# Softmax attention on one core: the scores of a head as two fp16 passes over projected queries and keys, in place of three passes over a folded product

## What is computed

```python
def _L1_attn_ref(hidden_states, w_q, w_k, w_v, w_o, rel_bias_table):   # 16 heads of 64
    q = shape(hidden_states @ w_q)
    k = shape(hidden_states @ w_k)
    v = shape(hidden_states @ w_v)
    scores = jnp.einsum('bhqd,bhkd->bhqk', q, k)
    scores = scores + position_bias
    attn = jax.nn.softmax(scores.astype(jnp.float32), axis=-1).astype(scores.dtype)
    ctx = jnp.einsum('bhqk,bhkd->bhqd', attn, v)
    return ctx.reshape(B, S, INNER) @ w_o
```

## Time and profile before

| quantity | value |
|---|---|
| median of three executions | 3229.51 us |
| the profiled execution, its own time | 3240.09 us |
| its span, first to last instruction | 3238.0 us |
| attention stage, about 1676 us to 3003 us of the span | 1327 us |
| busy in the span: TensorE, VectorE, ScalarE, GpSimd | 74%, 70%, 57%, 43% |
| mean granted TensorE clock | 0.903 |

### The profile page before, as it was taken

One profiled execution on the slowest core, in us unless ns is written; L12 is line 12 of the kernel. 1 busy time (PEld: TensorE's weight loads), 2 busy tenths in 40 slices (PEclk: granted clock), 3 DMA queues, 4 the chain that ended last, 5 costly groups with the idle time before them and its releaser, 6 DMA issues. The chain is left out here.

```text
span 3238.0 us, 66865 instructions
## 1 busy us (share of the span) xinstructions
PE 2386.1 (74%) x17707; PEld 1919.1 (59%) x17707; DVE 2265.8 (70%) x8247; ACT 1857.2 (57%) x4874; POOL 1401.3 (43%) x1366
## 2 busy tenths in 40 slices
PE   2217888384226787307868999999999999999587
PEld 2217676363225676305655877777777777778365
DVE  4325766685433666577977888888888888888697
ACT  2114444252213344235637988888888888889464
POOL 3553555302563555405532444444444444444365
PEclk9999999696558999758988999999999999999799
DMA  4133333312114333340000000000000000000000
GB/s 151 40 67 93 98 99 95 100 39 87 40 50 100 97 99 95 94 122 1 0 27 4 5 4 4 4 4 4 4 4 4 4 4 4 4 4 5 6 20 27
DMA packets 141736, 138.32 MB, mean 43 GB/s; under 512 B 17012, under 2 KB 127412, under 8 KB 140772
## 3 DMA queue, kind: packets, MB, share of 16 engines
q1 hardware_dynamic: 118932, 95.46, 9.8%
q0 software_dynamic: 17408, 35.82, 3.5%
q10 hardware_dynamic: 5200, 4.84, 0.5%
HBM read 59.31 MB, written 44.24 MB: 32 GB/s over the span
## 5 line engine op out<-in xcount | busy, mean ns | idle before, releaser
L2088 POOL TENSOR_TENSOR p_prob<-p_prob,p_inverse 128x512 f32<-128x512 f32 x512 | 533.3, 1042 | 797.0 <-DVE p_inverse L1912 797.0
L2005 ACT ACTIVATE p_prob<-p_neg,p_neg_max 128x256 f32<-128x256 f32 x1024 | 508.8, 503 | 40.2 <-DVE p_neg_max L1906 40.2
L1916 DVE SCALAR_TENSOR_TENSOR p_probT<-p_t_ps,p_probT 128x512 f16<-128x512 f32 x512 | 353.0, 689 | 195.1 <-ACT p_probT L2011 135.6
L883 ACT ACTIVATE p_e_hT<-p_e_h_ps,p_b 128x256 f32<-128x256 f32 x576 | 230.9, 474 | 352.9 <-PE p_e_h_ps L832 216.0
L997 POOL DMA_INDIRECT results_by_token<-p_e_result,p_e_slot x288 | 285.2, 990 | 309.6 <-DVE p_e_result L943 234.2
L706 POOL DMA_INDIRECT rows_by_expert<-p_r_z,p_r_target x256 | 249.4, 974 | 371.5 <-DVE p_r_z L561 258.2
L1906 DVE CUSTOM_DVE_ANT_0 p_neg<-p_s_ps,top_bias 128x256 f32<-128x256 f32 x1024 | 388.3, 416 | 0.8 <-ACT p_prob L2005 0.6
L2011 ACT ACTIVATE p_probT<-p_t_ps 128x512 f16<-128x512 f32 x512 | 304.9, 596 | 71.2 <-PE p_t_ps L2156 69.5
L841 PE MATMUL p_e_o_ps<-p_w,p_e_hT 128*128 x2304 | 308.2, 289 | 35.4 <-issue 22.7
L841 PEld LDWEIGHTS p_e_o_ps<-p_w,p_e_hT 128*128 128x128 f32 x2304 | 285.5, 201 | 55.9 <-issue 55.9
L2156 PE MATMUL p_t_ps<-top_ident,p_prob 128*128 128x128 f32 x2048 | 308.8, 273 | 7.0 <-POOL p_prob L2088 7.0
(11 more groups left out here) (266 smaller groups left out, 6157.3 us busy)
## 6 DMA issues: line engine op xcount, KB each, us to landing
p_e_affine<-p_affine SPq DMA_DIRECT2D x144, 192.0 KB
p_e_z<-rows_by_expert SPq DMA_DIRECT2D x144, 129.0 KB, 2.2
p_got<-results_by_token SPq DMA_DIRECT2D x64, 256.0 KB, 2.9
results_by_token<-p_e_result,p_e_slot POOLq DMA_INDIRECT x288
p_r_w<-in_w SPq DMA_DIRECT2D x2, 2048.0 KB, 7.6
p_w<-in_w SPq DMA_DIRECT2D x2, 2048.0 KB, 11.8
rows_by_expert<-p_r_z,p_r_target POOLq DMA_INDIRECT x256
p_reversed<-bias_by_distance ACTq DMA_DIRECT2D x2, 2048.0 KB, 17.1
```

What stands on the lines that cost most here:

```text
L1916: v.scalar_tensor_tensor(probT[k % 2][:, 1, :, :], t_ps[k % 2][:], PROB_SCALE, probT[k % 2][:, 0, :, :], ALU.mult, ALU.subtract).then_inc( ...
L2005: ins = act.activation(prob[k % PROBS][:, t, :], neg[k % 2][:, t, :], ACT.Exp, bias=neg_max[k % 2][:, t:t + 1], scale=-1.0, accum_out=tota ...
L2088: pool.tensor_tensor(prob[k % PROBS][:], prob[k % PROBS][:], inverse[k % PROBS][:].unsqueeze(2).to_broadcast([P, SEQ_TILES, SEQ]), ALU.mult)\
```

## The change

The folded matrix A and the operand gT are gone. Queries and keys are projected with the plain weights, two heads (a pair, 2 by 64 = 128 output rows) at a time: of a quad's eight projections, four are now Q and K of two pairs, four are the values as before. The banks and slots stay: `act_ps` takes Q0, Q1, V0, V2, `v_ps` takes K0, K1, V1, V3. The split into high and low parts and its two copies per projection stay too.

The scores of a head contract over 64 instead of 128. In `stacked` each head has its query high and low parts one above the other on 128 partitions, and its key high part twice. One pass of full height then gives high by high plus low by high; a second pass, of 64 rows, taken straight from `qkT`, adds high by low. The stacking is done by SyncE: four DMAs within SBUF (64 partitions by 512 fp16 columns, 64 KB) for Q and four for K of each pair, 16 a quad, 64 a group. SyncE waits for the copies out of PSUM before them, and TensorE waits at the first scores of each pair for `moved`, the semaphores of these DMAs. In the setup the 16 products for A and their copies are replaced by a split of the weights read from memory.

```diff
+FIRST_BANK = ((Q, 0), (Q, 1), (V, 0), (V, 2))
+SECOND_BANK = ((K, 0), (K, 1), (V, 1), (V, 3))
...
-        gT = [m.sb(f"gT{b}", [P, 2, QUAD, GN], F16) for b in range(2)]
+        qkT = [m.sb(f"qkT{b}", [P, 2, 2, QUAD_PAIRS, GN], F16) for b in range(2)]
+        stacked = [m.sb(f"stacked{b}", [P, 2, QUAD, GN], F16) for b in range(2)]
...
+            def move(of, pair, i, g):
+
+                here, there_ = qkT[g % 2], stacked[g % 2]
+                first, second = slice(0, D_HEAD), slice(D_HEAD, P)
+                for h, own in enumerate((first, second)):
+                    parts = (HIGH, LOW) if of == Q else (HIGH, HIGH)
+                    for part, to in zip(parts, (first, second) if h == 0 else (second, first)):
+                        sp.dma_start(there_[to, of, pair * 2 + h, :], here[own, part, of, pair, :]).then_inc(moved[of][pair], 16)
+
+            def stack_quad(i, g):
+
+                if not (first_group(i) and g < 2):
+                    sp.wait_ge(s_done, i * GROUP_UNITS + (g - 1) * UNITS)
+                    sp.sem_inc(carried, 1)
+                for pair in range(QUAD_PAIRS):
+                    sp.wait_ge(act_taken, g_ready(i, g, pair))
+                    sp.sem_inc(carried, 1)
+                    move(Q, pair, i, g)
+                    sp.wait_ge(v_taken, v_number(i, g, pair) + 1)
+                    sp.sem_inc(carried, 1)
+                    move(K, pair, i, g)
...
             for n in range(QUADS):
                 norms.raw(v, n * (TILES // QUADS), TILES // QUADS, x_res)
-                v.wait_ge(a_kept, 2 * n + 1)
-                v.scalar_tensor_tensor(a_low[:, a_heads(n), :], a_bank(n), A_SCALE, a_high[:, a_heads(n), :], ALU.mult, ALU.subtract).then_inc(a_kept, 1)
+            for of in (Q, K):
+                v.wait_ge(qk_split, 2 * of + 1)
+                v.scalar_tensor_tensor(wqk_low[:, of], wqk[:, of], A_SCALE, wqk_high[:, of], ALU.mult, ALU.subtract).then_inc(qk_split, 1)
...
+                pair = g * QUAD_PAIRS + n
+                return three_passes(out, (wqk_high[:, of, pair, :], wqk_low[:, of, pair, :]), (src[:, 0, :], src[:, 1, :]))
...
             def scores(i, k):
                 g, b, hd = quad_of(k), k % UNITS // QUAD, k % QUAD
-                if b == 0:
-                    pe.wait_ge(act_taken, g_ready(i, g, hd))
-                if k == UNITS:
-                    pe.wait_ge(key_ready, i * 16 + 16)
+                pair, half = hd // 2, slice(hd % 2 * D_HEAD, hd % 2 * D_HEAD + D_HEAD)
+                if b == 0 and hd % 2 == 0:
+                    for of in (Q, K):
+                        pe.wait_ge(moved[of][pair], (i * QUADS + (g + 1)) * 64)
                 if not early(i, k, 2):
                     pe.wait_ge(max_ready, i * GROUP_UNITS + (k - 1))
-                keys = zT if g == 0 else keyT
                 toks = slice(b * SEQ, (b + 1) * SEQ)
                 for t in range(SEQ_TILES):
                     rows = slice(b * SEQ + t * P, b * SEQ + (t + 1) * P)
-                    ins = three_passes(s_ps[k % 2][:, t, :], (gT[g % 2][:, 0, hd, rows], gT[g % 2][:, 1, hd, rows]),
-                                       (keys[:, 0, toks], keys[:, 1, toks]))
+                    pe.matmul(s_ps[k % 2][:, t, :], stacked[g % 2][:, Q, hd, rows], stacked[g % 2][:, K, hd, toks], start=True, stop=False)
+                    ins = pe.matmul(s_ps[k % 2][:, t, :], qkT[g % 2][half, HIGH, Q, pair, rows], qkT[g % 2][half, LOW, K, pair, toks],
+                                    start=False, stop=True)
                 ins.then_inc(s_done, 1)
```

More of the change, by code:

```diff
@@ L1639 @@
 A_SCALE = 2.0 ** 4
-G_SCALE = 2.0 ** 5
+QK_SCALE = 2.0 ** 5
 B_SCALE = 2.0 ** 4
@@ L1643 @@
 PROB_SCALE = 2.0 ** 15
-SCORE_SCALE = G_SCALE * Z_SCALE
+SCORE_SCALE = QK_SCALE * QK_SCALE
+QUAD_PAIRS = QUAD // 2
+Q, K, V = range(3)
+FIRST_BANK = ((Q, 0), (Q, 1), (V, 0), (V, 2))
+SECOND_BANK = ((K, 0), (K, 1), (V, 1), (V, 3))
 UNITS = GROUP_SEQS * QUAD
@@ L1789, in bias_attention @@
                                              for key in ("o_done", "o_kept", "o_turned", "o_added"))
-        a_done, a_kept, b_done, b_kept = m.sem("a_done"), m.sem("a_kept"), m.sem("b_done"), m.sem("b_kept")
+        qk_split, b_done, b_kept = m.sem("qk_split"), m.sem("b_done"), m.sem("b_kept")
+        moved = [[m.sem(f"{key}_moved{pair}") for pair in range(QUAD_PAIRS)] for key in ("q", "k")]
+        carried = m.sem("carried")
         high_ready, key_ready = m.sem("high_ready"), m.sem("key_ready")
@@ L1798, in bias_attention, with kept @@
         OUT_SCALE = 1.0 / (PROB_SCALE * VALUE_SCALE)
+        HIGH, LOW = range(2)
+        def kept(g, part, use):
+            of, n = use
+            return (val[g % 2][:, part, n, :], VALUE_SCALE / (Z_SCALE * B_SCALE)) if of == V else \
+                (qkT[g % 2][:, part, of, n, :], QK_SCALE / (Z_SCALE * A_SCALE))
         def last_group(i):
@@ L1884, in keep_keys, with group @@
                 sp.dma_start(keyT[:], zT[:]).then_inc(key_ready, 16)
-            loop_groups(sp, 0, GROUPS, keep_keys)
+            def move(of, pair, i, g):
[16 more added lines that the diff above has]
+                    move(K, pair, i, g)
+            def group(i, ahead):
+                keep_keys(i)
+                for g in range(1, QUADS):
+                    stack_quad(i, g)
+                if ahead:
+                    stack_quad(i + 1, 0)
+            stack_quad(0, 0)
+            group(0, True)
+            loop_groups(sp, 1, GROUPS - 1, lambda i: group(i, True))
+            group(GROUPS - 1, False)
         @block.vector
@@ L1927, in keep_low_z, with keep_low_first @@
                     .then_inc(act_taken, 1)
-            def keep_low_g(i, g, n):
+            def keep_low_first(i, g, n):
                 v.wait_ge(high_ready, g_number(i, g, n))
-                v.scalar_tensor_tensor(gT[g % 2][:, 1, n, :], act_ps[:], G_SCALE / (Z_SCALE * A_SCALE), gT[g % 2][:, 0, n, :],
-                                       ALU.mult, ALU.subtract).then_inc(act_taken, 1)
+                (high, scale), (low, _) = (kept(g, part, FIRST_BANK[n]) for part in (HIGH, LOW))
+                v.scalar_tensor_tensor(low, act_ps[:], scale, high, ALU.mult, ALU.subtract).then_inc(act_taken, 1)
             def add_output(i, b):
@@ L2057, in _ @@
             act.wait_ge(loaded, 64)
[L2058 to L2062, removed]
+            for of in (Q, K):
+                if of > 0:
+                    act.wait_ge(qk_split, 2 * of)
+                act.activation(wqk_high[:, of], wqk[:, of], ACT.Copy, scale=A_SCALE).then_inc(qk_split, 1)
             act.wait_ge(stats_ready, 1)
@@ L2116, in three_passes, with project, project_first, project_second @@
                 return pe.matmul(out, lhsT[1], rhs[0], start=False, stop=stop)
-            def project_g(g, n, number):
-                h = g * QUAD + n
+            def project(out, g, use):
+                src = zT if g <= 1 else keyT
+                of, n = use
+                if of == V:
+                    toks, heads = slice(n * P, (n + 1) * P), slice(g * QUAD, (g + 1) * QUAD)
+                    return three_passes(out, (src[:, 0, toks], src[:, 1, toks]),
+                                        (b_high[:, heads, :].rearrange("p h d -> p (h d)"), b_low[:, heads, :].rearrange("p h d -> p (h d)")))
+                pair = g * QUAD_PAIRS + n
+                return three_passes(out, (wqk_high[:, of, pair, :], wqk_low[:, of, pair, :]), (src[:, 0, :], src[:, 1, :]))
+            def project_first(i, g, n, number):
                 pe.wait_ge(act_taken, number)
-                src = zT if g <= 1 else keyT
-                three_passes(act_ps[:], (a_high[:, h, :], a_low[:, h, :]), (src[:, 0, :], src[:, 1, :])).then_inc(act_done, 1)
-            def project_v(i, g, n):
+                if g == 2 and n == 0:
+                    pe.wait_ge(key_ready, i * 16 + 16)
+                project(act_ps[:], g, FIRST_BANK[n]).then_inc(act_done, 1)
+            def project_second(i, g, n):
                 number = v_number(i, g, n)
@@ L2207, in _ @@
                     rows = slice(h % 2 * D_HEAD, h % 2 * D_HEAD + D_HEAD)
[L2208 to L2213, removed]
                     ins = pe.matmul(a_bank(n)[:, j, :], wvT[rows, h // 2, :], wo[rows, h // 2, :], start=True, stop=True)
```

67 lines of the change are left out of this document (33 added, 34 removed).

## The result

The changed kernel takes 3316.1 us (median of four executions, 3314.0 to 3331.7). The kernel before took 3229.0 in four executions beside it. The ratio is **1.027, interval 1.023 to 1.031**: 87 us slower where 100 us less were forecast. A later repeat on another chip gives 1.026.

What follows compares the result with a forecast made beforehand. TensorE, issuing without a gap at 2.39 us a unit in the attention stage, was taken as the bound. Sixteen groups give 94 us and the setup 6, so 3229.5 - 100 = 3129.5, or 3130 us; range 3108 to 3310.

Steps and rivals of the forecast that it cites:

- The pass that goes: Attention scores: four of six 256-column passes stay, height changes cost nothing, so a TensorE unit falls 0.22 us to 2.17.
- rival A: Score passes: four height changes a unit cost up to 0.16 us each, making the kernel slower, 3270 to 3420 us; 26%.
- The unit without the price: Attention stage: a TensorE unit of 2.39 - 0.22 = 2.17 us if height changes are free, TensorE still setting the pace.
- The turn of the loop: Group loop's turn: VectorE's pause stays, TensorE waits 2.6 us, plus 0.9 for little slack; 73.8 us a group, 5.9 less.
- The stacking DMAs: SyncE's copies for the scores: issue 0.465 us each, landing 2.2, hidden with 0.6 to 1.3 us to spare.
- Rival B: Stacked copies land late and TensorE waits at a pair's first scores; mostly 3160 to 3215 us in all; 10%.
- The setup: Start of the attention stage: statistics end 6.4 us sooner, first quad's copies may give back 0.5; 6 us less.
- The sum: Whole kernel: 94 us from sixteen groups plus 6 from the setup, 100 us less, giving 3130 us.

Runs made afterwards that it cites:

- experiment 2: Changed kernel with the second tile's score passes swapped (full, half, half, full), two height changes a unit instead of four; 3088.8 us, ratio 0.999 to the kernel before.
- experiment 1: Changed kernel with the second score pass on all 128 rows, stacked queries against both heads' low key parts; 3030.6 us, ratio 0.979 to the kernel before.
- experiment 3: As experiment 1, but the second pass of the even heads takes 96 rows, that of the odd heads 128; 3032.2 us, ratio 0.979 to the kernel before.
- Experiment 6: As experiment 1, but the first quad's stacking copies wait only for their own projections; 3176.3 us, ratio 0.978 to the kernel before on that chip.
- experiment 7: As Experiment 6, with 12 stacking DMAs a quad instead of 16; 3153.6 us, ratio 0.972 to the kernel before on that chip.

## Why the prediction was wrong

**The pass that goes: the failed step.** The prediction wrote "I take nothing, by the 96-row matmuls, which are nearest", between bounds of nothing and 0.16 for a change of height. The runs show 0.105 for each change to or from 64 rows (unit 2.59 in the changed kernel, 2.38 to 2.39 in experiment 2, 2.17 to 2.18 in experiment 1) and nothing for 96 rows (experiment 3). "Nearest" was measured in rows of the array, and that was the wrong measure: the text of rival A already said that 96 rows may be no change of mode at all, and the number was taken from them all the same. The other bound, 0.27 - 0.11 = 0.16 from the modelled end of a pass, was nearer. The bounds held.

**Rival A is what happened.** It named the place, the four changes and the point of 0.055 from which they decide, with a chance of 26%. By its own formula with the measured price: 32 x 2.59 + 0.9 is 83.8, and with the 0.9 that TensorE waits at a turn (11.1 us in 12) 84.7 us a group; 84.8 was measured. Its side remark, that the turn costs less when TensorE is slower, held only in part: some 0.7 of the drop came without a longer unit (experiment 2). The stated range took in a third of this rival's cases and ended at 3310, just below what was measured. The Trainium skill (TensorEngine Tiling (Array Packing), "Key Properties") says that a change of tiling mode drains TensorE; the traces agree that a change between 64 and 128 rows costs something, 0.10 us, and show no price for 96; whether it is a drain they do not show. The Trainium skill (TensorE: Matmul & The Clock Gate, Part 2) says that a weight load is pulled ahead of a running matmul when the row groups don't conflict or when it goes to the background buffer. The trace shows the pull-ahead within full height, 0.21 early beside a pass of 512 columns, and none across a change of height.

**The unit without the price** was right. 2.39 - 0.22 = 2.17 is the undisturbed unit of experiment 1 (2.17 to 2.18), and TensorE stays the bound in it: "TensorE still sets the pace, by little".

**The turn of the loop** was nearly right in size, in part by luck. With 12 DMAs, a group of 74.6 is 32 x 2.175 + 0.9 = 70.5 and 4.1 more; the forecast put 2.6 + 0.9 = 3.5 there, and about 0.4 of the 4.1 are late copies (6.2 us over 16 groups). That VectorE's pause stays, "since its program keeps its length", was wrong: it is two, together 3.7 in the changed kernel, a fifth shorter.

**The stacking DMAs.** The landing was right: 2.0 us for 64 KB in the pages of experiments 2 and 3, 2.2 forecast. The issue was mis-sized: 0.465 for one alone, 0.63 in a row. More than that, the chain counted only the four copies of one K. At 0.63 four of them are longer than a unit of 2.17, so the copies of Q and K of both pairs add up in the queue. Rival B, 10%, was therefore partly true of the fast version: 16 DMAs against 12 are 75.8 - 74.6 = 1.2 us a group, 19 in all. In the changed kernel itself the units of 2.59 are just longer than four copies, 2.5, and hide it.

**The setup.** The statistics gave 5.9 of the forecast 6.4. The "may give back 0.5" was 9.3: the first copies wait for `ACT_LEAD`, all four `act_ps` uses, in code that the prediction had before it. Experiment 6 got 7.0 of it back; most of the rest is the zT copy behind the 16 stacked ones in the queue.

**The sum.** Forecast 16 x 5.9 + 6 = 100 less; measured 16 x 5.1 + 3 more. Of the difference of 185 us, 0.42 x 32 x 16 = 215 are the changes of height. The turn that became cheaper than forecast takes back 16 x (3.5 - 0.9) = 42, and the setup adds 9. That is 182.

**What stays open.** The runs show that 96 rows cost nothing and 64 do; where between 64 and 96 rows the price begins, what a change between 64 and 32 rows costs, and what one from the upper to the lower 64 rows costs, was not tried. Nor was the rest of experiment 7's turn of 3.7 us: VectorE's pauses read "issue", and no run says what they are. Of the 87 us lost, about 2 lie in neither the setup nor the groups.

## What to carry to other kernels

A matmul on 64 rows between matmuls on 128 costs TensorE about as much time again as a pass of 256 columns (0.105 us against 0.109), twice: once going in and once coming out. Where saved work comes as half-height passes, fill the other half with data whose product does no harm, or put the half passes side by side; count the changes, not the rows. And where many small DMAs share one queue, compare the issue time of all that fall due in a unit with the unit, not only the chain of the last one.

## What the runs showed of the hardware

- **The price of a change of height is mostly a time, not a number of TensorE's cycles.** At the start of the stage the granted clock is 0.50, the 1.2 GHz level. First the changed kernel, then experiment 1:

```profile
1711.69 0.40 PE L2197 MATMUL p_s_ps<-p_stacked 128*128 128x256 f16 x1
1712.02 0.39 PE L2198 MATMUL p_s_ps<-p_qkT 64*128 64x256 f16 x1
```

```profile
1575.63 0.42 PE L2197 MATMUL p_s_ps<-p_stacked 128*128 128x256 f16 x1
1575.84 0.42 PE L2198 MATMUL p_s_ps<-p_qkT,p_stacked 128*128 128x256 f16 x1
```

  0.33 against 0.21 apart, 0.12 for the change. At the 2.4 GHz level it is 0.21 against 0.11, 0.10. The columns take twice as long, the change hardly longer.
- **Half the array saves no time.** A 64-row pass of 256 columns follows another in 0.12 us (experiment 2), no sooner than a full one follows a full one, 0.11.
- **A copy of 64 KB within SBUF** takes 2.0 us from issue to landing. Issued in a row such copies take SyncE 0.63 us each from start to start, 0.60 of it the copy's own row (median); a copy of 128 KB reads 0.62 (median in experiment 7), so fewer and larger copies are worth having.
